# A quantized down projection in seven integer products: four of eight blocks, with the operand sums made by VectorE

## What is computed

```python
scale = cond @ norm_w.T + 1.0
ms = jnp.mean(x * x, axis=-1, keepdims=True)
h = x * (scale[:, None, :] * jax.lax.rsqrt(ms + EPS))
u = h @ up_w.T
val, gate = jnp.split(u, 2, axis=-1)
h = val * jax.nn.gelu(gate, approximate=False)
hq = act_quant(h)        # clip(round(h * s), -128, 127) / s, s = 127 / max |h| of the token
wq = weight_quant(down_w)  # clip(round(w * t), -1, 1) / t, t = 1 / mean |w|
y = hq @ wq.T
return y + x
```

## Time and profile before

| | before |
|---|---|
| median of 3 runs | 743.75 us (743.3 to 743.89) |
| the profiled execution: its own time | 744.86 us |
| the profiled execution: span | 743.0 us |
| TensorE busy | 733.5 us (99%) |
| VectorE busy | 521.8 us (70%) |
| ScalarE busy | 337.3 us (45%) |
| down projection of blocks 0 to 6 (L716) | 448 matmuls of 512 columns |

### The profile page before, as it was taken

The page is one execution under the profiler, slowest core; times in us unless marked ns, Lnnn a source line. Parts: engine busy times, 40 slices in busy tenths (PEclk is TensorE's granted clock), DMA queues, the critical chain, the costliest instruction groups (busy, mean ns, idle before and its releaser), DMA issues.

```text
span 743.0 us, 14261 instructions
## 1 busy us (share of the span) xinstructions
PE 733.5 (99%) x5506; PEld 539.1 (73%) x5506; DVE 521.8 (70%) x1006; ACT 337.3 (45%) x662; POOL 104.8 (14%) x153
## 2 busy tenths in 40 slices
PE   6999999999999999999999999999999999999998
PEld 6544444444688887888778886788878887788864
DVE  5567777875889666876578855787568855577556
ACT  4788856442355533364234542355324443244410
POOL 1211477787330000000000000000000000000000
PEclk9999999999999999999999999999999999999999
DMA  8887574757545453343634344343543334353202
GB/s 313 289 279 230 187 271 147 260 169 257 207 146 160 143 194 123 118 151 102 198 99 154 117 141 156 113 157 101 162 143 104 101 100 134 115 181 108 90 29 86
DMA packets 44564, 117.60 MB, mean 158 GB/s; under 512 B 5584, under 2 KB 5840, under 8 KB 43344
## 3 DMA queue, kind: packets, MB, share of 16 engines
q1 hardware_dynamic: 44496, 116.68, 47.8%
HBM read 99.88 MB, written 16.79 MB: 157 GB/s over the span
## 4 chain that ended last, share of the span: by engine, by line
PE 97%; DMA 1%; DVE 0%; issue 0%; POOL 0%; SPq 0%; ACT 0%; DVEq 0%; POOLq 0%
PE ps_v L589 14%; PE ps_v L588 14%; PE ps_v L590 14%; PE ps_y L716 13%; PE ps_g L589 6%; PE ps_g L588 6%; PE ps_g L590 6%; PE ps_v L606 4%; PE ps_g L607 4%; PE ps_g L606 4%; PE ps_v L607 4%; PE ps_v L608 4%; PE ps_g L608 4%; PE ps_v L795 1%; DMA q<-in_up_t_dram 1%; PE ps_v L682 1%
## 5 line engine op out<-in xcount | busy, mean ns | idle before, releaser
L588 PE MATMUL ps_v<-x_hi,w_hi 128*128 128x256 f16 x968 | 263.9, 273 | 0.0
L589 PE MATMUL ps_v<-x_lo,w_hi 128*128 128x256 f16 x968 | 263.9, 273 | 0.0
L590 PE MATMUL ps_v<-x_hi,w_lo 128*128 128x256 f16 x968 | 263.9, 273 | 0.0
L814 ACT COPY ps_g<-ps_v 128x256 f32<-128x256 f32 x96 | 34.3, 357 | 208.2 <-PE ps_v L590 208.2
L825 ACT ACTIVATE g<-ps_g,w_unscale 128x512 f32<-128x512 f32 x128 | 87.3, 682 | 77.6 <-PE ps_g L590 73.5
L1146 DVE TENSOR_TENSOR ps_v<-ps_v,p 128x256 f32<-128x256 f32 x96 | 41.5, 432 | 113.2 <-PE ps_v L590 113.0
L588 PE MATMUL ps_g<-x_hi,w_hi 128*128 128x256 f16 x392 | 106.9, 273 | 0.2 <-DVE x_lo L1136 0.2
L589 PE MATMUL ps_g<-x_lo,w_hi 128*128 128x256 f16 x392 | 106.9, 273 | 0.0
L590 PE MATMUL ps_g<-x_hi,w_lo 128*128 128x256 f16 x392 | 106.9, 273 | 0.0
L589 PEld LDWEIGHTS ps_v<-x_lo,w_hi 128*128 128x128 f16 x968 | 94.7, 98 | 13.5
L588 PEld LDWEIGHTS ps_v<-x_hi,w_hi 128*128 128x128 f16 x968 | 94.7, 98 | 13.5
(11 more groups left out here) (137 smaller groups left out, 889.6 us busy)
## 6 DMA issues: line engine op xcount, KB each, us to landing
w_lo<-w_lo_dram SPq DMA_DIRECT2D x96, 448.0 KB, 3.3
q<-in_up_t_dram SPq DMA_DIRECT2D x16, 512.0 KB, 4.4
xt<-in_x_cols_dram SPq DMA_DIRECT2D x8, 1024.0 KB, 4.9
res<-in_x_rows_dram SPq DMA_DIRECT2D x26, 256.0 KB, 3.4
out_dram<-res SPq DMA_DIRECT2D x26, 256.0 KB, 2.7
xs<-in_x_rows_dram SPq DMA_DIRECT2D x22, 256.0 KB, 3.6
w_lo_dram<-w_lo SPq DMA_DIRECT2D x16, 256.0 KB, 4.3
dw<-in_down_t_dram SPq DMA_DIRECT2D x8, 512.0 KB, 6.5
```

The costliest lines, as they stand in the source:

```text
L588: pe.matmul(to, w_hi[:, wh:wh + P], hi, start=start and kt == 0, stop=False, skip_group_check=True)
L589: pe.matmul(to, w_hi[:, wh:wh + P], lo, start=False, stop=False, skip_group_check=True)
L590: last = pe.matmul(to, w_lo[:, wl:wl + P], hi, start=False, stop=(kt == 1), skip_group_check=True)
```

## The change

For blocks 2 to 5 (`D_SEVEN`) the down projection of four token tiles is done in two pairs of tiles, (0, 2) and (1, 3). A pair is a 2 x 2 product: two token tiles by two halves of each pair of hidden tiles, times two halves of the hidden tiles by two halves of 256 output columns. It is computed with seven products of 8 matmuls of 256 columns in place of 32 matmuls of 512 columns.

- POOL makes four weight terms (`d_t`, fp8, 2048 columns each) once, behind its last work.
- VectorE makes in iterations 3 to 10, behind the two quantized tiles, three sums or differences of 256 columns in fp16 (`sum_tokens`), for each pair of hidden tiles; the difference is written over a part of `q`. In two later iterations it makes one of 1024 columns (`sum_last`) and two adds of 256 columns through PSUM (`d_seed`, `d_second_low`).
- ScalarE copies two results of 256 columns out of the way for each pair of token tiles (`d_copies`), ahead of its other work of that iteration.
- TensorE's calls of a pair are spread over four iterations: `d_pair` at the end of the first, `d_second` ahead of `second(n)` in the next, `d_third` there and `d_gates` at the end in the third, `d_fourth` ahead of `second(n)` in the fourth. The first pair starts in iteration 11, the second in iteration 15, of the block after.
- The residual of a pair's first tile comes ahead of `seed_gate`, that of its second tile behind it, both in the fourth of these iterations (14, and 2 of the next block). SyncE loads the `x` tiles of the first pair in iteration 5 and stores both in 15, and of the second pair loads in 0 and stores in 3.

The core of the diff:

```diff
+    D_SEVEN = range(2, NB - 2)
+    D_START = 11
...
+    def d_chunk(n, since):
+        b, j = divmod(n - since, J)
+        b -= 1
+        return [(c, p) for c, p, at in ((b, 0, D_START), (b, 1, D_START + 4)) if c in D_SEVEN and j == at]
...
+                if b - 1 in D_SEVEN and j == 15:
+                    store_y(b - 1, 0)
+                    store_y(b - 1, 1)
+                if b - 2 in D_SEVEN and j == 0:
+                    load_res(b - 2, 2)
+                    load_res(b - 2, 3)
...
+            def d_product(to, left, right, start=False):
+                for k in range(NK):
+                    last = pe.matmul(to, left[:, k, :], right[:, k, :], start=start and k == 0, stop=k == NK - 1,
+                                     skip_group_check=True)
+                return last
...
+                for c, p in d_chunk(n, 1):
+                    d_second(c, p)
+                for c, p in d_chunk(n, 2):
+                    d_third(c, p)
+                for c, p in d_chunk(n, 3):
+                    d_fourth(c, p)
                 if seven:
                     second(n)
                 if seven_before:
...
-                if b >= 2 and j < 3:
+                for c, p in d_chunk(n, 0):
+                    d_pair(c, p)
+                for c, p in d_chunk(n, 2):
+                    d_gates(c, p)
+                if b >= 2 and b - 2 not in D_SEVEN and j < 3:
                     down(b - 2, j + 1)
...
+            def d_copies(b, p):
+                act.wait_ge(dp_ready, 2 * d_index(b) + p + 1)
+                act.copy(ps_y[:, 1, 0:HD], ps_y[:, 0, 0:HD]).then_inc(dp_copied, 1)
+                act.copy(d_copy[p], ps_y[:, 0, HD:D]).then_inc(dp_copied, 1)
...
+            def sum_tokens(b, k):
+
+                x = d_index(b)
+                base = 3 * (NK * x + K_ORDER.index(k))
+                a11, a21, a22 = q_parts[:, k, 0, 0], q_parts[:, k, 0, 1], q_parts[:, k, 1, 1]
+                dve.wait_ge(q_ready, b * J + Q_AT[2 * k + 1] + 1)
+                if x >= 1:
+                    dve.wait_ge(dv2_ready, 2 * x)
+                dve.tensor_tensor(d_s1[:, :, k, :], a21, a22, ALU.add).then_inc(ds_step, 1)
+                dve.wait_ge(ds_step, base + 1)
+                dve.tensor_tensor(a21, a11, a21, ALU.subtract).then_inc(ds_step, 1)
+                dve.tensor_tensor(d_s2[:, :, k, :], d_s1[:, :, k, :], a11, ALU.subtract).then_inc(ds_step, 1)
...
+                if b - 1 in D_SEVEN and tiles:
+                    sum_tokens(b - 1, tiles[0] // 2)
                 if n >= 2:
                     peak_of(n - 2)
-                if b >= 2 and j < 4 and n < NJ:
+                if b >= 2 and b - 2 not in D_SEVEN and j < 4 and n < NJ:
                     residual(b - 2, j, ps_y[:, j % 2, :])
+                for c, p in d_chunk(n, 3):
+                    residual(c, 2 * p, ps_y[:, 1, :])
                 if n < NJ and in_seven(n):
                     seed_gate(n)
+                for c, p in d_chunk(n, 1):
+                    d_seed(c, p)
+                    sum_last(c, p)
+                for c, p in d_chunk(n, 2):
+                    d_second_low(c, p)
+                for c, p in d_chunk(n, 3):
+                    residual(c, 2 * p + 1, ps_y[:, 0, :])
```

More of the change, by code:

```diff
@@ L138, in h_home, with d_index, y_row @@
         return J + j if j < 2 and b % 2 == 1 else j
+    D_SEVEN = range(2, NB - 2)
+    D_START = 11
+    HD = D // 2
+    NK = J // 2
+    K_ORDER = [*range(1, NK), 0]
+    PAIR = ((0, 2), (1, 3))
+    def d_index(b):
+        return b - D_SEVEN[0]
+    def d_chunk(n, since):
+        b, j = divmod(n - since, J)
+        b -= 1
+        return [(c, p) for c, p, at in ((b, 0, D_START), (b, 1, D_START + 4)) if c in D_SEVEN and j == at]
+    def y_row(b, k):
+        return PAIR[k // 2][k % 2] if b in D_SEVEN else k
     with ExitStack() as ctx:
@@ L545, in _ @@
                         load_rs(c)
-                if b >= 1 and j in (14, 15):
+                if b >= 1 and b - 1 not in D_SEVEN and j in (14, 15):
                     load_res(b - 1, j - 14)
-                if b >= 2 and j < 4:
+                if b >= 2 and b - 2 not in D_SEVEN and j < 4:
                     if j in (1, 2):
@@ L718, in down, with d_low, d_high, d_pair @@
                 last.then_inc(y_ready, 1)
+            def d_product(to, left, right, start=False):
[3 more added lines that the diff above has]
+                return last
+            def d_low(half):
+                return ps_y[:, 0, half * HD:(half + 1) * HD]
+            def d_high(half):
+                return ps_y[:, 1, half * HD:(half + 1) * HD]
+            def d_pair(b, p):
+                x = d_index(b)
+                if x == 0 and p == 0:
+                    pe.wait_ge(dt_step, 4)
+                pe.wait_ge(ds_step, 3 * NK * (x + 1))
+                pe.wait_ge(y_done, b * TT + 2 * p)
+                d_product(d_low(0), q_parts[:, :, 0, 0, p, :], d_b[:, :, 0, 0, :], start=True)
+                d_product(d_low(1), d_s1[:, p], d_t[:, 0]).then_inc(dp_ready, 1)
+            def d_second(b, p):
+                pe.wait_ge(dp_copied, 2 * (2 * d_index(b) + p + 1))
+                d_product(d_low(0), d_s2[:, p], d_t[:, 1]).then_inc(du2_ready, 1)
+            def d_third(b, p):
+                pe.wait_ge(dg_seeded, 2 * d_index(b) + p + 1)
+                d_product(d_low(0), q_parts[:, :, 0, 1, p, :], d_t[:, 2]).then_inc(du3_ready, 1)
+            def d_gates(b, p):
+                d_product(d_high(0), q_parts[:, :, 1, 0, p, :], d_b[:, :, 1, 0, :])
+                pe.wait_ge(ds4_ready, 2 * d_index(b) + p + 1)
+                d_product(d_high(1), q_parts[:, :, 0, 0, p, :], d_b[:, :, 1, 1, :]).then_inc(y_ready, 1)
+            def d_fourth(b, p):
+                pe.wait_ge(dv2_ready, 2 * d_index(b) + p + 1)
+                d_product(d_low(0), q_parts[:, :, 1, 1, p, :], d_t[:, 3]).then_inc(y_ready, 1)
             pe.wait_ge(consts_loaded, 32)
@@ L777, in _ @@
                     spread_scale(b - 1)
-                if b >= 1 and j == J - 1 and n + 1 != 2 * J:
+                if b >= 1 and b - 1 not in D_SEVEN and j == J - 1 and n + 1 != 2 * J:
                     down(b - 1, 0)
@@ L1029, in _, with down_terms @@
                 sum_weights(k)
+            def down_terms():
+                b11, b12, b21, b22 = [d_b[:, :, i // 2, i % 2, :] for i in range(4)]
+                pool.wait_ge(ws_ready, J)
+                pool.tensor_tensor(d_t[:, 0], b12, b11, ALU.subtract, saturate=False).then_inc(dt_step, 1)
+                pool.wait_ge(dt_step, 1)
+                pool.tensor_tensor(d_t[:, 1], b22, d_t[:, 0], ALU.subtract, saturate=False).then_inc(dt_step, 1)
+                pool.tensor_tensor(d_t[:, 2], b22, b12, ALU.subtract, saturate=False).then_inc(dt_step, 1)
+                pool.wait_ge(dt_step, 2)
+                pool.tensor_tensor(d_t[:, 3], b21, d_t[:, 1], ALU.subtract, saturate=False).then_inc(dt_step, 1)
+            down_terms()
         @block.vector
@@ L1242, in residual @@
                 u = y_tile(b, i)
+                r = y_row(b, i)
                 late = u - (NB * TT - 6)
```

44 lines of the change are left out of this document (41 added, 3 removed).

## The result

The changed kernel takes 751.70 us (median of 4 runs, 750.77 to 752.74) where the kernel before takes 743.58 (743.3 to 743.89): 1.0107 times as long, with a 95% interval of 1.0094 to 1.0120. The profiled execution of after took 750.97 us, its span is 749.2 us.

A forecast was written before the change was run, and what follows sets the result against it. TensorE's columns were taken to bound the kernel unless it waits. 13.8 us of waits for VectorE against 6.3 us saved gave +7.5 us on 743.75, so 751.2 us, with an 8 in 10 range of 746.5 to 763.5.

The forecast's parts named there:

- TensorE's saving: Down projection of four blocks: 64 matmuls of 512 columns become 112 slots of 256, 1.57 us a block, 6.3 in all.
- The adds: VectorE, iterations 3 to 10: three fp16 adds of 256 columns, 0.28 us each, ahead of `h_max`, making TensorE wait.
- S: VectorE's time for the three adds with their waits, per iteration: 0.84 us, with bounds of 0.48 and 1.24.
- the first rival: The fp16 adds run at one column a step, S = 1.24: +18.8, 762.6 us; chance 0.12.
- the second: Rival: the adds cost little more than their fixed part, S = 0.48: +1.2, 745.0 us; chance 0.09.
- The wait on the own engine: VectorE: a dependent instruction starts 0.03 us after its predecessor's end, an independent one 0.08 before; a wait costs some 0.12.
- The chain of latenesses in iterations 3 to 8: TensorE's waits because VectorE is late: 0.48 in block 3's iteration 3, then 0.41, 0.38 and 0.41 us.
- The estimate of 0.19 us an add: The skill's VectorE formula, 58 cycles and half the columns, applied to one fp16 add of 256 columns: 0.19 us.
- Iteration 2: TensorE waits at `fourth` for `second_val`, the moved residual ahead of it: 1.48 us in blocks 4 to 6, 0.87 in 7.
- What costs nothing: ScalarE's copies, POOL's subtractions and SyncE's loads and stores: taken to be covered, adding no time.
- my bound of 9.2: POOL's four subtractions of 2048 columns: 9.2 us each, 37 in all, first user about 100 us later.
- The third: Rival: iteration 2's moved residual does not bind, VectorE being earlier than set: 741.7 us; chance 0.07.

The follow-up runs named there:

- act_order: The changed kernel with ScalarE's cast of the first x difference moved from iteration 2 to 3, behind the up projection's copies: 751.01 us.
- sums_behind_seed: The changed kernel with the three fp16 adds of iterations 3 to 10 moved from ahead of `h_max` to behind `seed_gate`: 748.49 us.
- adds_alone: The kernel before with VectorE's 24 fp16 adds a block added in iterations 3 to 10 of four blocks, results unused: 749.55 us.
- no_adds: The changed kernel without VectorE's fp16 sums and their waits, products reading quantized tiles in their place: 747.56 us.
- pool_later: act_order with POOL's four subtractions held back to the end of the loop's block 2: 763.60 us.
- residual_later: act_order with the fourth token tile's residual moved from iteration 2 to 9, its store and tile load later too: 748.28 us.

## Why the prediction was right, and where it wasn't

The forecast was 751.2 us, the result 751.7, and +7.5 us in both sums. The sum comes out through terms that were too high and one that was missing, and 0.7 us of the result are the clock's (act_order, whose runs show no fall, takes 751.0); so the closeness is partly chance. By its steps:

**TensorE's saving: right.** The steps of iterations 11 to 2 are those worked out from the slot, to 0.01 us, and the four blocks give 6.32 us for 6.3. That these iterations are free for VectorE's `sum_last` (0.68 us, forecast 0.6) and the products through PSUM was right too.

**The adds: right, size and place.** The middle between two bounds, 0.28 us, was 0.29; S was 0.85 for 0.84. Fp16 adds at one column a step, the first rival, would have taken 0.41, adds at their fixed part, the second, 0.16; the means of the three lines are 0.292, 0.292 and 0.284. The twofold rate that the Trainium skill (VectorE: DVE Perf Modes, "The perf-mode tier table") gives for `tensor_tensor` on bf16 in SBUF is what these fp16 rows show: 768 columns more take 0.39 us more, 0.51 ns each, where an fp32 add of the earlier trace rows takes 0.26 us for 256. The wait on the own engine held as well: 0.04 us from the end of the first add at 393.31 to the start of the second at 393.35. The chain of latenesses in iterations 3 to 8 was forecast at 0.48, 0.41, 0.38, 0.41 and measured at 0.42, 0.34, 0.40, 0.34; sums_behind_seed took them all away and adds_alone made them on the other kernel. The estimate of 0.19 us an add in the prediction, which its sum did not use, was too low by a third.

**Iteration 2: the right amount in the wrong place.** 2.48 us were forecast for iterations 2 and 3, at `fourth` for `second_val` and at `third` for `seed_gate`; 2.39 were measured, 2.24 of them at `second`, for ScalarE. The step that failed is in "What costs nothing". It asked of ScalarE only what the new copies add: 0.36 us each under the 1.31 us of the first pair, and 1.97 us for the up projection's copies. It did not ask what else stands ahead of those copies in ScalarE's queue, and whom that waits for. The trace of before had the answer in its waits of ScalarE:

```profile
ACT x_hi L867 <- DVE ta L1116: 16.0, 6, 3.5
```

Six times ScalarE stood for the difference, up to 3.5 us, with the down tile's 3.45 us as cover. The change took that cover away from ScalarE's copies as it did from `second_val`. The sum was right nonetheless, because both routes hang on the same row of VectorE's work, as act_order showed. But the place has a price of its own, the next point.

**A fall of the clock: not in the sum.** A wait of 2.2 us at one time is followed in a part of the executions by some 3.4 us at half clock, 1.67 us each, where two waits of 1.36 and 1.00 are not. It lifts the median of after by about 0.7 over act_order's, and that of no_adds by 1.7 over what its other steps give. With the wait split over the two places where I had put it, none of act_order's four runs shows it.

**POOL: the step that failed outright.** Four subtractions at 3.8 to 4.3 us each were shorter than my bound of 9.2, and their user was far away, both as I said. To list them under "What costs nothing" was wrong: they cost 0.92 us. I had asked who waits for POOL's result and when POOL comes free, and not what POOL's instruction keeps others from doing while it runs. The price depends on which of VectorE's instructions stand beside it: 0.92 at iteration 7 of block 2, 13.7 at its end, 2.6 of them through the clock. The Trainium skill (SBUF — State Buffer, "Who interferes with whom") states that VectorE's instruction with two inputs in the SBUF contends with a GpSimd instruction that reads the SBUF, and that their shared pair of ports is an exclusive lock. The rows of pool_later agree, 4.3 us a `low` for 0.68 alone beside subtractions of some 4 us; I had not drawn on it.

**The rivals.** The third, that the move of the residual doesn't bind, is excluded by residual_later: 0.64 us a block come from that move, in the very place. Its time of 741.7 us was also worked out short: 0.5 us a block over the four blocks with adds is 2.0 and not 1.5. That the waits came to 13.8 us as forecast is partly chance: 0.92 us of POOL were missing, and the terms of iterations 2 to 8 were too high by 0.18 in block 3, 0.21 in each of blocks 4 to 6 and 0.09 in block 7, 0.9 together. By steps the terms held within 0.1 us each.

**What stays open.** Why the clock falls in one execution and not in another with the same wait: the microsecond before the restart shows TensorE at 0 in both, and the moment of the fall differs, 0.77, 0.01 and 0.11 us after the restart in the three that were recorded. And the 1.26 us by which the start-up of the two profiled executions differs, in a part that the change doesn't touch. That POOL and VectorE exclude each other is shown by durations and by both moves of POOL's work; that it is the second SBUF input which does it rests on which of VectorE's instructions were stretched; no run isolates it.

## What to carry to other kernels

When work is taken from the engine that bounds the kernel, list the waits of every other engine in that stretch, not the new ones alone: what it covered, also of queues that the change doesn't touch, comes to light, here a cast that ScalarE had always waited for. Put new VectorE work behind the instruction whose result the bounding engine waits for: with that order, the residual, the cast and the preparation of x moved out of iteration 2, and POOL's work in pieces, the change that cost 8.1 us gained 4.7. The order alone was not enough (sums_behind_seed, still 4.9 us above before). And give a long POOL instruction to an iteration only after looking at which VectorE instructions with two SBUF inputs run beside it, or cut it in pieces shorter than the slack there.

## What the runs showed of the hardware that I had not expected

POOL and VectorE, both with two inputs in the SBUF, ran in turns: 4 `low` of 0.68 us took 4.3 us each beside POOL's subtractions of 3.9 to 4.3, and one `h_max` 2.36, while instructions of VectorE with an input in PSUM kept their time. In pieces of 256 columns POOL takes 0.64 us each, up to 1.11 where it meets `h_max`, and `h_max` at most 1.11.

TensorE's granted clock went to 0.50 within 0.8 us of its restart from a wait of 2.2 us, and stayed there for 3.4 us, in 2 of 3 such places in one profiled execution, in 1 of 3 in another, in 0 of 3 in that of after; in the profiled executions whose longest wait there is at most 1.4 us no step shows it. In a wait of 11 us (pool_later) it fell while TensorE stood, 2.8 us in, and it came back 5.2 us after the restart.
